# A decoder layer on one core: DMA transposes for the self attention's probabilities, their high parts written by ScalarE, a reordered first stage, and the residual's copy and addition moved

## The reference, cut to what matters

```python
# first block: a state space layer, 32 heads of 16
xp = x @ W_in.T;  dt = softplus(xp @ W_dt.T + b_dt)
a = exp(dt[..., None] * -exp(log_A));  ys[t] = a[t] * ys[t-1] + xp[t]
x = layernorm(x + ys @ W_out.T)
# cross attention: 16 heads on 8 key/value heads, 1024 keys, mask, head size 128
p = nan_to_num(softmax(where(mask, q @ k.T / sqrt(128), -inf)))
x = layernorm(x + (p @ v) @ Wo)
# block 3: RMS norm, then causal self attention, 16 heads on 4 key/value heads, 512 keys, RoPE on q and k
h = x + (softmax(causal(q @ k.T / sqrt(128))) @ v) @ wo        # q, k, v from rmsnorm(x)
# then RMS norm, a gate that takes the best 2 of 8 experts, silu(x w1) * (x w3) @ w2, weighted sum
```

## Time and profile before

| | us |
|---|---|
| median of 3 runs | 1588.07 (1587.24 to 1590.05) |
| the profiled execution | 1587.12 |
| its span, first to last instruction | 1585.4 |
| busy: PE, DVE, ACT, POOL | 1417.2, 1073.2, 671.1, 566.2 |
| stages: phase_ssm, xa, n2, sa, n3, route, MoE | 0 to 87.5, to 712.5, to 740, to 1124, to 1148, to 1163, to 1585 |

### The profile page before, as it was taken

How to read it: one execution, slowest core, us unless ns; L and a number is a source line. 1 busy time by engine, 2 the same in 40 slices (tenths; PEclk the granted TensorE clock), 3 DMA queues, 4 the chain that set the end, 5 groups by cost and what they waited for, 6 DMA issues and landing times. The chain is left out here.

```text
span 1585.4 us, 25071 instructions
## 1 busy us (share of the span) xinstructions
PE 1417.2 (89%) x8371; PEld 774.6 (49%) x8371; DVE 1073.2 (68%) x1980; ACT 671.1 (42%) x1336; POOL 566.2 (36%) x725
## 2 busy tenths in 40 slices
PE   7988999999999999974889999998569999999981
PEld 3343544444444444432455566664246666666640
DVE  4757787777778778757677777775575655555554
ACT  4534444444434444313355645555244444444420
POOL 6314243434343333325674746553450000000124
PEclk9999999999999999995999999999779999999986
DMA  9226667576766575747010020000426454455233
GB/s 260 47 56 123 140 110 149 111 147 113 145 115 143 107 151 107 132 93 277 1 59 10 1 67 0 26 1 1 166 81 240 174 189 146 185 195 192 97 91 119
DMA packets 339126, 181.08 MB, mean 114 GB/s; under 512 B 287440, under 2 KB 301776, under 8 KB 339056
## 3 DMA queue, kind: packets, MB, share of 16 engines
q1 hardware_dynamic: 335280, 169.72, 42.3%
q0 software_dynamic: 3200, 10.49, 2.1%
q10 hardware_dynamic: 576, 0.00, 0.0%
HBM read 90.33 MB, written 18.55 MB: 69 GB/s over the span
## 5 line engine op out<-in xcount | busy, mean ns | idle before, releaser
L1081 ACT ACTIVATE xa_SC<-xa_SC,xa_mn 128x1024 f32<-128x1024 f32 x128 | 147.1, 1150 | 211.6 <-DVE xa_mn L1177 211.6
L1164 DVE SCALAR_TENSOR_TENSOR xa_PN<-xa_SC,xa_rs,xa_PN 128x1024 f16<-128x1024 f32 x128 | 190.4, 1487 | 58.9 <-issue 58.2
L973 PE MATMUL xa_psS<-xa_KT,xa_QT 128*128 128x512 f16 x768 | 186.4, 379 | 4.8 <-DVE xa_mn L1177 3.4
L985 PE MATMUL xa_psO<-xa_PT,xa_V 128*128 128x512 f16 x768 | 172.3, 381 | 10.6 <-DMA xa_PT<-xa_PN 10.6
L907 POOL TENSOR_SCALAR xa_rs<-xa_rc,flag 128x1 f32<-128x1 f32 x128 | 33.9, 265 | 383.8 <-DVE xa_rc L1186 383.8
L1177 DVE CUSTOM_DVE_ANT_0 xa_SC<-xa_psS,maskb 128x1024 f32<-128x1024 f32 x128 | 155.4, 1214 | 13.5 <-PE xa_psS L973 8.9
L909 POOL TENSOR_SCALAR xa_PN<-xa_SC,xa_rc,flag 128x1024 f16<-128x1024 f32 x128 | 152.1, 1188 | 0.1
L2038 PE MATMUL rmoe_psU<-rmoe_XGT,W 128*128 128x352 f16 x768 | 127.2, 314 | 7.0 <-issue 6.9
L1580 ACT ACTIVATE sa_SC<-sa_SC,sa_mn 128x128 f32<-128x128 f32 (+3 forms) x128 | 71.9, 562 | 134.9 <-DVE sa_mn L1676 134.9
L2038 PE MATMUL rmoe_psG<-rmoe_XGT,W 128*128 128x352 f16 x768 | 126.5, 315 | 2.2 <-DVE rmoe_XGT L2121 1.5
L2053 PE MATMUL rmoe_psY<-W,rmoe_HT 128*128 128x512 f16 (+1 forms) x576 | 126.8, 379 | 0.0
(11 more groups left out here) (236 smaller groups left out, 2592.9 us busy)
## 6 DMA issues: line engine op xcount, KB each, us to landing
W13raw<-in_L_ffn_w_dram SPq DMA_DIRECT2D x16, 2048.0 KB, 11.7
W2raw<-in_L_ffn_w_dram SPq DMA_DIRECT2D x8, 2048.0 KB, 8.4
expert_rows_dram<-zeros SPq DMA_DIRECT2D x11, 512.0 KB, 8.9
xa_WPraw<-in_L_xattn_Wq_dram SPq DMA_DIRECT2D x8, 512.0 KB, 4.9
xa_WOraw<-in_L_xattn_Wo_dram SPq DMA_DIRECT2D x8, 512.0 KB, 4.7
sa_WPraw<-in_L_ffn_wq_dram SPq DMA_DIRECT2D x4, 1024.0 KB, 6.3
sa_WOraw<-in_L_ffn_wo_dram SPq DMA_DIRECT2D x4, 1024.0 KB
expert_out_dram<-rows SPq DMA_DIRECT2D x16, 256.0 KB, 2.0
```

What stands on the lines that cost most here:

```text
L973: last = nc.tensor.matmul(psS[j % 2][:, c:c + cw], QT[b][:, hq, g, t * P:(t + 1) * P], KT[b][:, hk, c:c + cw], start=(q == 0), stop=(q == 2))
L985: last = nc.tensor.matmul(psO[:, c:], V[b][:, hv, blk, :], PT[g % NPT][:, blk, hp, c:], start=(blk + q == 0), stop=(blk == NBLK - 1 and q ...
L1081: nc.scalar.activation(SC[j % 2][:, 0:w], SC[j % 2][:, 0:w], ACT.Exp, bias=mn[:, j % 4:j % 4 + 1], scale=-1.0, accum_out=sm[:, j % 4:j % 4 ...
L1164: nc.vector.scalar_tensor_tensor(out=PN[j % NPN][:, 0:w // P, 1, :], in0=by_block(SC[j % 2], w), scalar=rs[:, j % 4:j % 4 + 1], in1=PN[j % ...
```

## The change

1. **phase_ssm**: XN, its copies and its four DMA transposes are gone; batch 1's x is turned by PE (16 more transposes, four more jobs of `split_banks`) after the fused gate. Both gates run before the later projections, their abs and exp for both batches, then ln for both, then the splits. Spread 0 comes in two parts between projections. Accumulators are assigned anew.
2. **n2 and n3**: the copy X to X2 is 8 DMAs on SP behind `fetch`, and the stage waits for them. The addition X += X2 leaves n3 and stands at the end of POOL's program in `phase_route`.
3. **sa** runs through `attention` as well, and `attention_by_tensor` is deleted: PN is written as high and low f16 parts (ACT, DVE), SP turns it by `dma_start_transpose`. There it has four score buffers (NSC), the reciprocal one step (SUM_LAG) and the low part two steps (LOW_LAG) later, PT in 2 buffers, PN in 4, values 6 steps after the scores (TAIL), their low part one more (VLAG).
4. **xa**: the high part of PN, POOL's L909, is written by ACT (`split_high`), one step later and ahead of that step's exponential; POOL keeps the scale rs. The wait for the landed transpose moves from POOL to ACT. POOL's scale waits for the low part of three steps before. The three accumulators of the jobs are taken by the tables BANK and BACK.

```diff
@@ attention
+    BANK = (0, 1, 2, 0, 1, 2, 0, 1, 2, 1)
+    BACK = (3, 2, 3, 3, 3, 3, 3, 3, 3, 2)
+    VLAG = 1 if causal else 0
     NPN = 4
-    NPT = 4 if causal else 2
+    NPT = 2
+    NSC, SUM_LAG, LOW_LAG = (4, 1, 2) if causal else (2, 0, 1)
@@ its gpsimd
                     pool.wait_ge(recip_done, n + 1)
-                    if j >= NPN or not first:
-                        pool.wait_ge(landed[j % TPB], 16 * (head_of(h, j - NPN) + 1))
+                    wait_from(pool, split_done, n - 3)
 ...
                     nc.gpsimd.tensor_scalar(rs[:, j % 4:j % 4 + 1], rc[:, j % 4:j % 4 + 1], unit, 1.0, ALU.mult,
                                             ALU.mult).then_inc(scale_done, 1)
-                    nc.gpsimd.tensor_scalar(PN[j % NPN][:, 0:w // P, 0, :], by_block(SC[j % 2], w), rc[:, j % 4:j % 4 + 1],
-                                            unit, ALU.mult, ALU.mult).then_inc(norm_done, 1)
@@ its tensor
-                wait_from(pe, masked, n - 1)
+                wait_from(pe, masked, n - NSC + 1)
 ...
-                        project(h + 1, 1 - b, i, job, psJ[k % NJ], back)
+                        project(h + 1, 1 - b, i, job, psJ[BANK[k]], BACK[k])
@@ its scalar
+            def split_high(h, m, first):
+                n, j = h * NS + m, m % NS
+                w = width(j % TPB)
+                act.wait_ge(scale_done, n + 1)
+                if m >= NPN or not first:
+                    act.wait_ge(landed[j % TPB], 16 * (h * groups + (m - NPN) // TPB + 1))
+                nc.scalar.activation(PN[j % NPN][:, 0:w // P, 0, :], by_block(SC[j % NSC], w), ACT.Identity,
+                                     scale=rs[:, j % 4:j % 4 + 1]).then_inc(norm_done, 1)
 ...
                     if j in short:
                         jobs(h, b, j, first, last, 0)
+                    if not causal and j <= NS and (j or not first):
+                        split_high(h, j - 1, first)
                     if j < NS:
 ...
                     if j not in short:
                         jobs(h, b, j - LAG, first, last, 0)
+                    m = j - SUM_LAG
+                    if causal and m < NS and (m >= 0 or not first):
+                        split_high(h, m, first)
@@ its vector
-                        wait_from(dve, norm_done, n - 1)
-                        wait_from(dve, split_done, n - 1)
+                        wait_from(dve, norm_done, n - NSC + 1)
+                        wait_from(dve, split_done, n - NSC + 1)
 ...
-                    if j <= NS and (j or not first):
-                        split_low(n - 1, (j - 1) % NS)
+                    m = j - SUM_LAG
+                    if causal and m < NS and (m >= 0 or not first):
+                        reciprocal(n - SUM_LAG, m)
+                    m = j - LOW_LAG
+                    if m < NS and (m >= 0 or not first):
+                        split_low(n - LOW_LAG, m % NS)
@@ phase_norm
+            if keep is not None:
+                for i in range(NT):
+                    sp.wait_ge(ln_done, i + 1)
+                    sp.dma_start(keep[:, i, :], X[:, i, :]).then_inc(kept, 16)
+                sp.wait_ge(kept, 16 * NT)
 ...
-                if 0 <= n < NT and keep is not None:
-                    nc.gpsimd.tensor_scalar(keep[:, n, :], X[:, n, :], 1.0, 1.0, ALU.mult, ALU.mult)
-                if 0 <= n < NT and add is not None:
-                    pool.wait_ge(xw_done, n + 1)
-                    nc.gpsimd.tensor_tensor(X[:, n, :], X[:, n, :], add[:, n, :], ALU.add)
@@ phase_route, gpsimd
             nc.gpsimd.tensor_copy(earlier16[:], earlier[:]).then_inc(mats_done, 1)
+            for i in range(NT):
+                nc.gpsimd.tensor_tensor(X[:, i, :], X[:, i, :], X2[:, i, :], ALU.add)
@@ phase_ssm, tensor
             fused_gate()
-            project(0, 2)
+            for n in range(first_jobs, len(jobs)):
+                tr_pe(pe, n)
             pe.wait_ge(wz_lo, 1)
             gate(0)
+            pe.wait_ge(tr_lo, len(jobs))
+            gate(1)
             project(0, 3)
-            pe.wait_ge(x1_turned, 16 * TPB)
+            project(0, 2)
             project(1, 0)
-            gate(1)
             pe.wait_ge(sel_done, 1)
-            spread_steps(0)
+            spread_steps(0, (0, 1))
             project(1, 1)
+            spread_steps(0, (2, 3))
             project(1, 2)
             project(1, 3)
-            spread_steps(1)
+            spread_steps(1, range(DC))
@@ decoder_layer
-            attention_by_tensor(nc, "sa", X, XT, XT, identF, weights, wq, wk, wv, wo, 4, 4, S,
+            attention(nc, "sa", X, XT, XT, identF, weights, wq, wk, wv, wo, 4, 4, S,
```

## The result

The changed kernel takes 1571.32 us (1570.18 to 1574.32, 4 runs), the kernel before beside it 1588.74: ratio 0.9892, interval 0.9876 to 0.9908, so 17 us or 1.1% faster. The forecast was 1539, 49 us faster. The sign holds and the time lies in the wide range (1518 to 1576), but the gain is a third of what was forecast. The profiled execution took 1574.32 with a span of 1571.8, 13.6 less than the span before.

The account below looks back on a forecast made before the run. TensorE was taken to bound cross and self attention, 64% of the span; DMA bounds n2, DVE and POOL chains n3 and routing. Terms -4 - 10 + 8 - 38 - 4 = -48 from 1588.07 gave 1539 us, own range 1528 to 1552, wide 1518 to 1576.

Parts of the forecast that it names:

- Part 1: First stage: removed copies and DMA transposes outweigh added PE transposes; -4 us, ends -6 and -1, last spread near 50.
- Part 2: Cross attention: ACT writes the high part, POOL's weight piece comes earlier, PE's gaps shrink; -10 us, upper end +6.
- Rival A: Cross attention: ACT's in-order execution of the added high part lengthens the stage; 1552 to 1562 us in all, chance 0.12.
- Part 3: Norm n2: eight copy DMAs queue behind loads and zeroing, and the stage waits for them; +8 us, ends +4 and +12.
- Part 5: Norm n3 and routing: moving POOL's additions shortens n3 about 7.8 us and costs routing +4; net -4, ends -8 and +1.
- Part 4: Self attention: PE transposes leave, DMA transposes replace them, halves fall to 39.8 us; -38 us, ends -47 and -20.
- 43.4 less 4.4 is 39.0: Self attention: PE's 43.4 us a half loses 40 transposes of 0.11 us each, 4.4 us, leaving 39.0.
- for hiccups: Self attention: 0.8 us a half added to 39.0, giving 39.8, as more buffers and lags take the chain off the path.
- last half's -12: Self attention's last half, without projections: four score buffers cut its chain from 42 us to 29 to 32; -12 us.
- +1 for the tail: End of the self attention: one more transposed group costs +1 us.
- rival C: Self attention: DVE's low parts queue behind whole POOL operations, 47.9 us a half; about 1610 us in all, chance 0.08.
- B: Rival: self attention bound by DVE, slowed by POOL contention, halves about 42 to 43 us; 1555 to 1580 in all, chance 0.13.

Follow-up runs that it names:

- experiment 5: Changed kernel with the whole first stage (phase_ssm) of the kernel before put back: ratio 0.9880 to the kernel before; first stage 90.8 us.
- experiment 6: Changed kernel without the OT lag and with POOL's X copy, plus self-attention probability low parts for the first 128 keys only: ratio 0.9721, a half 38.98 us.

## Why the prediction was right and wrong

**Part 1, first stage (-4): not borne out, not refuted.** It came out as +2.0 and -0.7 in two profiles against the first one of before, and as -1.0 to -4.0 against the old stage run beside it (experiment 5); the ratios with and without it are equal within some 5 us. The mean over all traces is 88.9 changed (12) and 89.1 old (2). The wait for XT went as forecast, and the scans of batch 0 start about where they did (42.63, before 41.84). What the walk missed is that PE, early now, waits for them: 4.28 us in the first profile, 2.64 in the second. So the last spread begins at 53.9 and 51.6, not near 50.

**Part 2, cross attention (-10): right** in mechanism and nearly in size, -7.9. The price of the new activation, the new end of the weight piece and the remaining gap are as worked out. The ends of the stage, for which I added 2 us, gave nothing. By the Trainium skill ("ScalarE: Activation LUTs", What ACT_TABLE_LOAD costs) the activation is 1.13 us, an estimate from its figures; the trace agrees within 2%, 1.149. Rival A didn't happen: PE waits 5.0 us for DVE's masks and 10.3 for turned tiles in the whole stage (3.4 and 10.6 before), and the stage is shorter.

**Part 3 (+8): right**, +6.9. The DMAs were issued in 0.96 us each, not 1.29, which saved 2.6 us; from the end of their issue to the next stage it took 3.7, not 2.6.

**Part 5 (-4): right**, -3.2, by its two terms -7.7 and +4.5.

**Part 4, self attention (-38): the step that failed.** The term "43.4 less 4.4 is 39.0" is right: experiment 6 measures 38.98. The 0.8 us a half "for hiccups" is what was mis-sized: it is 2.95 us in the first profile (41.95 - 39.0). The runs name 1.3 (the wait for OT's low part, 41.3 to 40.0), 1.0 (part of DVE's work, 40.0 to 39.0) and 0.65 (the low clock in the first profile, 41.95 to 41.3, with PE idle 8.8 us in both). Over five halves the miss is 10.8 us. The false step is the "so the chain is off the path" that the 0.8 rests on, and the error behind it was to look at sums of busy time and not at positions. The sum itself came out even better than taken: DVE is busy 32.6 us a half (162.80 in five), where I had put 36. But the change says that the low part of OT comes one step later (VLAG), the kernel before had its output job at the same step 8, and I never asked who waits for that lag. The prediction names the waits that the change takes away, not this one that it adds.

The last half's -12 was the other miss, with its +1 for the tail: the forecast for the stretch from the last mark was -13, and it moved by -1.3 in the first profile, -4.0 in the second, and -1.1 to -1.4 in the three others with this code. Without the lag it is -5.3 to -5.5, so some of this miss is the lag's too. I read the window of the earlier trace rows as a chain that four buffers dissolve, down to PE's load. But the values of a group still come after mask, exponential, reciprocal, scale, high part, low part, issue and landing, and with nothing else for PE to do this latency lies open twice, 4.3 and 6.1 us. At the very end it was shorter before: PE's last transposes with gaps of 1.32 and 1.40 us stood in the place of queue and landing. Now DVE's last low part ends at 1093.60 and the values start at 1097.23, 3.6 us later, where I had put +1 for one more transposed group. What fills the 4.3 us gap was not taken apart. The first stretch of the stage (-1.2 where -6.1 was forecast) looks alike: gaps of 4.43 us, which outlasts the lag's removal, and 2.06 for the weight piece, where PE had waited 5.6 in five places before.

Two slips of the working changed little. The terms of part 4 add up to -37.1 (-21.6 - 2.5 - 12 + 1 - 2), not -38. And in rival C a half of 47 us would make the stage 29 us longer (8 x 3.6), not 6.

**Rivals B and C.** The measured 1571 lies in B's range (1555 to 1580), and the halves of 41.95 come near its 42 to 43. That is luck: B's cause was DVE slowed by POOL to 40 us of work a half, and DVE has 32.6, where it had 32.4 before. Nor is DVE's work free, as experiment 6 shows; it is worth 1.0 us of the 2.95. C fell: the low parts took 74.9 us in all where the turned ones had taken 62.5, 1.6 us a half, not 16. By the Trainium skill ("SBUF — State Buffer", SBUF: two separate sides) each such operation, with two inputs in SBUF, can be shut out for a whole POOL operation that reads SBUF; the rows of the norm agree. In these halves it is rarely felt: the widest low parts took 0.814 us in the mean, where one in the quiet tail took 0.75 (at 1092.85), though POOL has some 14 large operations a half:

```profile
L1188 DVE SCALAR_TENSOR_TENSOR sa_PN<-sa_SC,sa_rs,sa_PN 128x512 f16<-128x512 f32 x32 | 26.0, 814 | 9.4 <-issue 7.4 <-ACT sa_PN L1076 1.4
```

## What to carry to other kernels

When a change takes work off the bound engine, that engine arrives earlier everywhere: list each thing that it will now wait for, with the time by which it was ready before, and above all every lag that the change adds elsewhere; the sum of busy times doesn't show it. Count the slack in the time of the engine that waits, not in steps of the loop. At both ends of a software pipeline, where the filling work is missing, the latency of a longer chain lay open here, though it had more buffers.

## What the runs showed that I had not expected

- An idle PE of 2.1 to 2.4 us is followed by twelve matmuls in 4.0 to 4.4 us in some halves and in 2.76 in others of the same execution (granted clock 0.62 to 0.66 over them in the first profile, 1.00 over the others); filling the gap kept it at 2.76 and shortened the half by no more than 0.3 us.
- The same code's self attention took 367.3 to 375.0 us in five profiles, and the experts' stage 408 and 420 in different groups of runs; what makes the experts' stage differ was not looked into.
- DMA transposes in the self attention occupy SP for 1.21 us in the median, in the cross attention, on tiles of 1024 keys in place of 320 on average, for 1.91.
